# A decoder layer on one core: the context's transposes and products for all batches at once, the similarity without its gamma columns, the last expert pair taken as single experts, and a new order on every engine

## What is computed

```python
# 1: linear attention with decay, 16 heads of 16, chunks of 128 tokens
q, k, v = rotary(ln(x) @ Wq), rotary(ln(x) @ Wk), ln(x) @ Wv
inter = (q * q_decay) @ kv_state
intra = ((q @ k.T) * dmask) @ v
x = x + rms_norm(inter + intra, rms_w) @ Wo
# 2: cross attention; p is the normalised x
kv = ctx @ W_k.T + b_k
out = p @ kv
sim = (out @ kv.T) * 256 ** -0.5
sim = (sim - mean(sim)) * rsqrt(var(sim) + EPS) * ln_gamma + ln_beta
x = x + softmax(sim)
# 3: experts; the gates are zero but for the two best experts of a token
h = ln(x)
x = x + sum(gate[e] * (h @ We[e] + be[e]) for e in range(8))
```

## Time and profile before

| | us |
|---|---|
| median of 3 runs | 134.36 |
| lowest and highest of them | 133.79, 134.41 |
| profiled execution, its own time | 134.21 |
| span of that execution in the trace | 131.9 |

### The profile page before, as it was taken

The page is one execution under the profiler, slowest core; times in us unless marked ns, Lnnn a source line. Parts: engine busy times, 40 slices in busy tenths (PEclk is TensorE's granted clock), DMA queues, the critical chain, the costliest instruction groups (busy, mean ns, idle before and its releaser), DMA issues.

```text
span 131.9 us, 2701 instructions
## 1 busy us (share of the span) xinstructions
PE 121.6 (92%) x1027; PEld 96.6 (73%) x1027; DVE 106.6 (81%) x327; ACT 59.3 (45%) x161; POOL 41.8 (32%) x54
## 2 busy tenths in 40 slices
PE   0599989969999999999999999999999999999990
PEld 0587866848768786975868998756888788887860
DVE  0848571999999785999699888999999779969972
ACT  3458789986530893565757011228940020010000
POOL 8030553999997332230404102334040000000000
PEclk9999999999999999999999999999999999999999
DMA  3999894000000000000000000001002001010012
GB/s 109 330 290 353 276 367 130 5 2 0 5 0 0 5 0 0 5 0 0 5 0 5 0 2 0 0 0 38 6 0 80 0 0 40 2 45 0 0 40 80
DMA packets 8028, 7.32 MB, mean 55 GB/s; under 512 B 2232, under 2 KB 7888, under 8 KB 7888
## 3 DMA queue, kind: packets, MB, share of 16 engines
q1 hardware_dynamic: 7792, 7.07, 16.4%
q10 hardware_dynamic: 224, 0.08, 0.3%
HBM read 6.11 MB, written 1.05 MB: 54 GB/s over the span
## 4 chain that ended last, share of the span: by engine, by line
PE 69%; DVE 16%; DMA 6%; SPq 4%; issue 3%
PE low L1362 28%; PE high L1362 11%; DMA xin<-in_x 6%; DVE probs L880 6%; PE low L1413 4%; PE high L1372 4%; PE high L1448 3%; PE high L1430 3%; PE high L1465 3%; PE high L1476 3%; DVE qk L868 2%; DVE rot_a L864 2%; PE high L1458 2%; PE low L1406 2%; PE low L1430 2%
## 5 line engine op out<-in xcount | busy, mean ns | idle before, releaser
L980 DVE SCALAR_TENSOR_TENSOR acc<-low,gate_x,acc 128x256 f32<-128x256 f32 x52 | 23.3, 478 | 3.0 <-PE low L1362 2.7
L880 DVE TENSOR_TENSOR probs<-low,dec 128x1024 f32<-128x1024 f32 x16 | 19.0, 1215 | 4.4 <-PE low L1413 4.4
L1362 PE MATMUL low<-w_e_hi,h3T_hi 128*128 128x512 f32 x52 | 17.1, 411 | 0.0
L1362 PE MATMUL low<-w_e_hi,h3T_lo 128*128 128x512 f32 x52 | 16.4, 396 | 0.0
L1362 PE MATMUL low<-w_e_lo,h3T_hi 128*128 128x512 f32 x52 | 16.3, 393 | 0.0
L386 POOL TENSOR_TENSOR w_e_lo<-w_e,w_e_hi 128x512 fp32r<-128x512 f32 x8 | 11.7, 1485 | 0.0
L1362 PEld LDWEIGHTS low<-w_e_lo,h3T_hi 128*128 128x128 f32 x52 | 9.8, 188 | 2.4
L1362 PEld LDWEIGHTS low<-w_e_hi,h3T_lo 128*128 128x128 f32 x52 | 9.8, 188 | 2.4
L1362 PEld LDWEIGHTS low<-w_e_hi,h3T_hi 128*128 128x128 f32 x52 | 8.9, 189 | 2.1 <-DVE acc L980 0.8
L1413 PE MATMUL low<-qx,kT 32*128 32x256 f32 x128 | 9.2, 400 | 0.0
L1362 PE MATMUL high<-w_qkv_hi,xT_hi 128*128 128x512 f32 (+1 forms) x32 | 8.9, 358 | 0.0
(11 more groups left out here) (186 smaller groups left out, 288.4 us busy)
## 6 DMA issues: line engine op xcount, KB each, us to landing
w_e<-in_L_ffn_We SPq DMA_DIRECT2D x2, 1024.0 KB, 11.0
xin<-in_x SPq DMA_DIRECT2D x4, 256.0 KB, 5.0
dec<-in_decay SPq DMA_DIRECT2D x1, 1024.0 KB, 8.4
out<-acc SPq DMA_DIRECT2D x8, 128.0 KB, 1.7
w_qkv<-in_L_attn_Wq SPq DMA_DIRECT2D x1, 256.0 KB, 3.2
w_qkv<-in_L_attn_Wk SPq DMA_DIRECT2D x1, 256.0 KB, 3.6
w_qkv<-in_L_attn_Wv SPq DMA_DIRECT2D x1, 256.0 KB, 4.4
cin<-in_ctx SPq DMA_DIRECT2D x1, 256.0 KB, 4.8
```

What stands on the lines that cost most here:

```text
L880: ve.tensor_tensor(probs[:, t, i, :], low[:, 2 * i:2 * i + 2, :].rearrange("p a n -> p (a n)"), dec[:, i, :], ALU.mult).then_inc(s_scores_ ...
L980: ve.scalar_tensor_tensor(out=acc[b % 2][:, t, :], in0=bank(n)[:, (e % 2) * D:(e % 2 + 1) * D], scalar=gate_x[b % 2][:, t, e:e + 1], in1=a ...
L1362: mm = pe.matmul(dst, a[:, c, a_cols], w[:, c, b_cols], start=(n == 0 and c == 0), stop=(n == 2 and c == KC - 1))
```

## The change

- **Context at once.** W_k is loaded twice side by side, by two DMAs of ACT's queue, so that its transpose stands in both halves of the partitions. `ctx_T` makes four full 128 x 128 transposes into one bank, `ctx_out` copies them at once, `kv_product` is two products of 512 columns (all batches; tile 0 from rows 0 to 63, tile 1 from rows 64 to 127) into two banks, and `kvT_out(b)` takes its 2 x 128 columns out of that pair. `kv_T` transposes 128 rows instead of 64, and `kv_out` drops the doubled half.
- **Loads.** The two b_k loads go from SP's queue to ACT's.
- **Similarity without gamma.** `kvS` holds only the centred keys, `kv_gamma` is gone, `similarity` takes 256 columns, and `sim_scale` goes to Vector, where one instruction multiplies the PSUM result by the per-token scale and by gamma.
- **Last expert pair as single experts.** For batch 3, experts 6 and 7 are two products of 256 columns (`unit_one`) with counters of their own, for both tiles.
- **Keep-clock** products: 2, 1 and 1 in three places instead of 5 in one.
- **Order.** The lists of all five engines are written anew.

The core of the diff:

```diff
-                    mm = pe.transpose(bank(n)[0:DC, t * P:(t + 1) * P], cin[:, b, t, :], ident)
+                for b in range(B):
+                    mm = pe.transpose(bank(n)[:, b * P:(b + 1) * P], cin[:, b].rearrange("p t d -> p (t d)"), ident)
-                pe.matmul(bank(n)[:, 0:T], w_ctxT[:], ctxT[b % 2][:], start=True, stop=True).then_inc(s_kv_product, 1)
+                    half = slice(t * DC, (t + 1) * DC)
+                    mm = pe.matmul(pair(n)[:, t, :], w_ctxT[half, :], ctxT[half].rearrange("p b n -> p (b n)"), start=True, stop=True)
-                    mm = pe.transpose(bank(n)[:, c * DC:(c + 1) * DC], kvS[b][0:DC, 0, c * P:(c + 1) * P], ident[0:DC, 0:DC])
+                    mm = pe.transpose(bank(n)[:, c * P:(c + 1) * P], kvS[b][:, c * P:(c + 1) * P], ident)
-                    mm = pe.matmul(bank((n0, n1)[t]), pkvT[b % 2][half, :], kvS[b][half, :, :], start=True, stop=True)
+                    mm = pe.matmul(bank((n0, n1)[t])[:, 0:T], pkvT[b % 2][half, :], kvS[b][half, :], start=True, stop=True)
-            def kv_gamma(b):
-                gp.tensor_tensor(kvS[b][:, 1, :], kvS[b][:, 0, :], gam[:], ALU.mult).then_inc(s_kv_gamma, 1)
-            def sim_scale(b, t, n):
-                act.activation(z[b % 2][:, t], bank(n)[:, T:], ACT.Copy, scale=sim_rs[b % 2][:, t:t + 1]).then_inc(s_sim_scale, 1)
+            def sim_scale(b, t, n):
+                ve.scalar_tensor_tensor(out=z[b % 2][:, t], in0=bank(n)[:, 0:T], scalar=sim_rs[b % 2][:, t:t + 1], in1=gam[:],
+                                        op0=ALU.mult, op1=ALU.mult).then_inc(s_sim_scale, 1)
+            def unit_one(b, e, t, n):
+                split_product(bank(n)[:, 0:D], h3T_hi[b % 2], h3T_lo[b % 2], w_e_hi, w_e_lo, slice(t * P, (t + 1) * P),
+                              slice(e * D, (e + 1) * D)).then_inc(s_unit_one, 1)
+            def unit_one_add(b, e, t, n):
+                ve.scalar_tensor_tensor(out=acc[b % 2][:, t, :], in0=bank(n)[:, 0:D], scalar=gate_x[b % 2][:, t, e:e + 1],
+                                        in1=acc[b % 2][:, t, :], op0=ALU.mult, op1=ALU.add).then_inc(s_unit_one_add, 1)
...
-            unit(2, 3, 0, 2)
+            unit(3, 2, 0, 2)
+            pe.wait_ge(s_unit_one_add, 1)
+            unit_one(3, 6, 0, 0)
+            pe.wait_ge(s_unit_one_add, 2)
+            unit_one(3, 7, 0, 1)
```

## The result

| | before | after |
|---|---|---|
| median of 4 runs, us | 134.07 (133.78 to 134.41) | 132.54 (131.97 to 133.82) |
| ratio, 95% interval | | 0.988 [0.984, 0.993] |
| profiled execution, its own time | 134.21 | 132.99 |
| its span | 131.9 | 131.2 |

The change is faster by 1.2%, where 3.3% was forecast; the median lies just above the range's upper end.

The account below looks back on a forecast made before the run. TensorE's work, its stalls and both ends were taken to bound the kernel. -1.1 - 0.65 - 1.7 + 0.1 - 0.5 - 0.5 = -4.35 against 134.21 gave 129.9 us, range 128.3 to 132.5.

Parts of the forecast that it names:

- start, first product's beginning: TensorE's start: the first q and k product begins at 9.0 instead of 10.14, -1.1 us, bounds -0.4 to -1.2.
- rival C: TensorE's clock rises late; first q and k product and context pair cost double, +1.4 and +1.06; chance 0.12, at 132.0.
- context products: On TensorE, one side-by-side pair of 512 columns (1.06 us) replaces three products of 256 columns (1.7): -0.65 us.
- similarity: On TensorE, half the columns take each of four similarities from 1.06 to 0.63 us: -1.7, bounds -1.1 and -1.9.
- last pair and tail: Kernel's end: single experts cost TensorE +0.1 us; one addition instead of two behind its last product gives -0.5.
- stalls: TensorE's waits for Vector: more other work from 27 to 43 us covers them, -0.5 us, bounds -2.0 and +2.5.
- Both end before their users want them: 0: Two b_k loads and the second W_k on ACT's queue, ahead of its first cast: no cost.
- The bound of 0.7 for a late context: At the start, x's low part or the context coming 0.7 us late would leave a gain of only 0.4.
- B: Vector becomes the bound behind 43 us; half to all of the scalings' 3.2 us returns as waits; chance 0.20, at 131.6.
- D: Slower: each of four scaling pairs on Vector waits uncovered for GpSimd's power, 6.8 us in all, 136.7; chance 0.06.
- E: The context pair doesn't run side by side and costs 1.9 us instead of 1.06, time 130.7; chance 0.08.
- the covers named: Vector work ahead of each batch's scalings (score half, gates, additions) hides the wait for GpSimd's power, some 0.9 us.

Follow-up runs that it names:

- e3: The changed kernel with Vector's att_low(0) moved ahead of batch 3's rotate_add and of square_add(0); 130.08 us.
- e0: The changed kernel run again with no edit; 132.37 us.
- e15: The changed kernel with the b_k loads on SP and W_k loaded once, attT_lo in its place as in the change; 130.95 us.
- e13: The e12 kernel with TensorE also waiting, idle, for the third x load before the context transposes; 132.36 us.
- e10: The e3 kernel with the b_k loads on SP and W_k loaded once, GpSimd writing the second copy; 129.79 us.
- e1: The changed kernel with the two b_k loads back on SP's queue; 131.83 us.
- e12: The e10 kernel run again with no further edit, as yardstick; 130.20 us.
- e14: The e13 kernel with the same added wait, but eight more keep-clock products ahead of it; 130.70 us.
- e9: The e3 kernel with the two b_k loads back on SP's queue; 130.80 us.
- e6: The e3 kernel with each of the eight scalings on Vector done twice, the extra one into a spare tile; 132.65 us.
- e4: The changed kernel with W_k loaded once and the second copy made by GpSimd; 134.2 us (before 134.28).

## Why the prediction was wrong

The sum by its own terms, from the profiled executions (spans; forecast -4.35, measured 131.2 - 131.9 = -0.7):

| term | forecast | measured | off by |
|---|---|---|---|
| start, first product's beginning | -1.1 | +0.8 | 1.9 |
| clock in the first product (rival C) | 0 | +0.9 | 0.9 |
| context products | -0.65 | -0.65 | 0 |
| similarity | -1.7 | -1.5 | 0.2 |
| last pair and tail | -0.4 | -0.4 | 0 |
| stalls | -0.5 | +0.6 | 1.1 |

The last column adds up to 4.1, and 3.65 are missing; the 0.45 between them has the size of what e3 showed, where taking 1.70 of stall away gave only 1.0, and isn't traced further. Product for product the arithmetic held to 0.2; what failed is waits and what they bring. The tail came out at its price by another path than mine (four additions in a row, above).

This is an execution with the wait for the context. In e0's profile, without it, 129.6 - 127.55 = 2.05 are missing, and there the stalls (1.1) and the clock (0.8) weigh more than the start (0.5). In the medians the loads put right are worth 1.4 (e0 to e15) and the order 0.75 to 1.0, together most of the 2.6 between 132.54 and 129.9.

**The step that failed first** is the last sentence of the part-by-part reckoning, "Both end before their users want them: 0", on the two b_k loads and the second W_k on ACT's queue. I asked when those loads would end, and they did end in time. I didn't ask what they do to the other loads in flight. They slowed them from 347 to 220 GB/s, so that the context landed after 6.9 us instead of 4.8, while the change at the same time wants it earlier (7.7 instead of 8.06). "The context has been there since 8.06 at the latest" was read from a kernel whose DMAs were different ones. The bound of 0.7 for a late context was in the right place and too small: TensorE stood 1.28 in the profile, and the idle time of e13 cost more than its length. Had the loads been as before, the step was right: e15 has its first product at 8.76, e10 at 8.72, against the forecast's 9.0.

**The start's smaller error** is W_k: I added one issue (0.52) to 4.67, but the second copy landed 1.0 later (5.65; 5.5 to 7.0 over the profiles). Loading it once gives 4.95 to 5.02.

**Rival C** (clock rises late, 0.12) came true in part: 0.9 in the first product, nothing in the context pair. Its reason, that transposes replace keep-clock products, doesn't decide by itself: e1, e12 and e14, with the same transposes, have first products of 1.59, 1.66 and 1.88. An idle stretch in front adds to it (e13: 2.84), which I had not thought of; why e9 took 2.65 without one stays open. As for the rule that I had cited, of the Trainium skill (TensorE: Matmul & The Clock Gate, Part 4: PE-mode transpose), no run here separates transposes from other work.

**The stalls are the second step that failed.** They were priced at -0.5 with bounds of -2.0 and +2.5, from a count of work per stretch: three more microseconds of cover for TensorE. That cover did its work: the longest wait for a rotation's result went from 1.23 to 0.32. What the count can't see is the order on Vector: `att_low` had been moved behind two score halves, a rotation and a sum, and TensorE came to a product that needs its bank. I had even named this wait ("attend(1, 0) now waits for att_low(1)") and not followed it through Vector's list. Part of its size is the sum of squares in front, which took 1.48 us beside GpSimd's instruction and 0.41 without. The Trainium skill (SBUF — State Buffer, SBUF: two separate sides) has a Vector instruction with two SBUF inputs, as this one, blocked by a GpSimd instruction that reads SBUF and was first; these rows agree.

**Rivals B, D and E.** TensorE has no stall behind 44.74, so B and D didn't come; the covers named did hide the scalings. But e6 shows the slack to be about 1.4 us (3.1 added, 1.7 through), not 6, and to lie in four places of 0.3 to 0.4 each: the mean share of an engine over 87 us says little. E is refuted by the 1.06 of the pair.

**The range** was narrower than its own terms. What it calls "the bounds of its own terms", 128.3 to 131.5, is not their sum: the lower bounds add up to 127.8 and the upper ones to 134.5, and the stalls' +2.5 alone gives 132.9. By its terms the sum allowed for what came; the stated upper end of 132.5 did not.

**Similarity** was priced 0.2 too high: two of the four stood back to back before and shared the entry of 0.2.

**What remains.** With the loads as before and `attT_lo` first, the kernel takes 129.79 us (e10) and 130.20 (e12), 0.967 [0.963, 0.970] and 0.973 [0.969, 0.977] of before: the forecast's 129.9, with the order mended too. That it comes so close is in part luck: in e10's profile the start (-1.4) and the stalls (1.47 in all, -0.8) are 0.3 better each than forecast, the first product (+0.5) and the similarity (-1.5) worse by as much. It beats both kernels.

## What to carry to other kernels

When a load is moved to another queue, cost it by what it does to the loads that others wait for, not by its own landing: look which transfer is wanted next, and keep tiny pieces behind it. Where a stage is short of cover, follow the releaser of each new wait through its engine's list, instruction by instruction; a sum of work per stretch does not show it. And before believing a difference, find a milestone behind which the profiles agree: here the stretch behind the second score tile agreed within 0.1 us in all profiles with the same work behind it but one (e4, 1.5 longer at the lower clock), and so one profile could price an edit that six timed runs couldn't, with such an exception as the risk.

## What the runs showed of the hardware

- Two loads of 256 bytes in pieces of 4 bytes, issued at 1.8 to 2.4 us on ACT's queue beside SP's large ones, went with 196 to 240 GB/s on the core's DMAs from 5 to 8 us (nine profiles) instead of 342 to 353 with the same loads at 5.0 to 5.2 us on SP's queue (nine profiles). The 256 KB load in flight landed after 5.2 to 6.9 us instead of 4.2 to 5.2.
- An empty wait of 1.33 us at the start cost 2.2 us in the median and 2.4 in the profile, the same wait filled with unneeded products 0.5 and 1.5. In one profile (e4) the granted clock stood at 0.50 to 0.52 from 45 to 48 us, behind the 1.70 wait, and the rest was 1.5 us longer; five other profiles with that wait didn't show it.
- A 256-column sum on Vector from SBUF took 0.41 us alone and 1.48 us beside a long GpSimd instruction (e0, e1 and e15: 1.48 too; e3, with the sum behind that instruction: 0.41).
- A product with four instructions in two halves of the rows, reading 64 rows each, runs side by side when its results cover all 128 rows of two banks: 1.06 us for four of 512 columns, 0.63 for four of 256.
